# A ring of four patch buffers for the gathers of a deformable convolution, filled a pair of blocks ahead

## The reference, cut to what matters

```
def reference(x, ...):                       # x: 8 x 256 x 128 x 128, float32
    x = x + L0(groupnorm(x))                 # layer 0
    x = x + L1(groupnorm(x))                 # layer 1
    return x

def L0(x, offset_w, offset_b, mod_w, mod_b, kv_w, kv_b, out_w, out_b):
    offsets = conv2d(x, offset_w, offset_b, 1)             # 3x3, 8 channels
    mod = 1.0 + tanh(conv2d(x, mod_w, mod_b, 1))           # 3x3, 4 channels
    v = conv2d(x, kv_w, kv_b, 0)[:, C:]                    # 1x1, 256 channels
    # px, py: each pixel's own place plus its offsets, one pair for each of 4 groups
    sampled = bilinear(v, px, py) * mod                    # four corners, weighted
    return conv2d(sampled, out_w, out_b, 0)                # 1x1

def L1(x, weight, bias):                     # whitening in 16 groups of 16 channels
    xg = (x - mean(x)) in groups
    cov = xg xg^T / M + 1e-4 I
    return (cov^(-1/2) xg) * weight + bias
```

## Time and profile before

| | us |
|---|---|
| median of 3 timed runs | 6903.72 |
| lowest, highest | 6898.48, 6908.78 |
| span of the profiled execution | 7542.0 |
| GpSimd busy in it | 4578.9 (61%) |
| TensorE busy (matmul) | 4572.0 (61%) |
| VectorE busy | 4223.0 (56%) |
| ScalarE busy | 1067.2 (14%) |

### The profile page before, as it was taken

How to read it: one execution, slowest core, us unless ns; L and a number is a source line. 1 busy time by engine, 2 the same in 40 slices (tenths; PEclk the granted TensorE clock), 3 DMA queues, 4 the chain that set the end, 5 groups by cost and what they waited for, 6 DMA issues and landing times.

```text
span 7542.0 us, 73500 instructions
## 1 busy us (share of the span) xinstructions
PE 4572.0 (61%) x17916; PEld 2935.6 (39%) x17916; DVE 4223.0 (56%) x8110; ACT 1067.2 (14%) x2723; POOL 4578.9 (61%) x4115
## 2 busy tenths in 40 slices
PE   5765656565566656655665656566665544446777
PEld 3443434344344433333443434343443333234322
DVE  6655656555565555555655556555555544345555
ACT  1211111111111111111111111111111111010000
POOL 0377667676767767667676677676776777770000
PEclk9877778787788878777887878787887766667999
DMA  8866657666666666666666666565565544445999
GB/s 283 275 203 212 200 185 227 195 205 201 197 206 207 209 194 208 197 193 207 202 216 196 201 206 217 188 216 186 184 195 183 187 131 136 129 129 193 421 421 412
DMA packets 1069670, 1612.36 MB, mean 214 GB/s; under 512 B 92080, under 2 KB 617008, under 8 KB 1067568
## 3 DMA queue, kind: packets, MB, share of 16 engines
q0 software_dynamic: 196608, 537.13, 22.2%
q10 hardware_dynamic: 632832, 536.91, 22.0%
q1 hardware_dynamic: 240176, 537.77, 20.7%
HBM read 1074.58 MB, written 536.87 MB: 214 GB/s over the span
## 4 chain that ended last, share of the span: by engine, by line
another core or an unknown queue 21%; issue 21%; PE 19%; DVE 18%; DMA 9%; POOL 5%; DVEq 3%; ACT 3%; ACTq 1%; POOLq 0%; SPq 0%
PE psA L929 6%; DVE patch L568 5%; PE psO L965 5%; POOL patch L829 5%; DMA out_dram<-vring 4%; DVE patch L570 4%; PE psG L994 3%; DMA vring<-x 3%; PE psT L954 2%; DVE xr L582 2%; DMA v<-vring 1%; DVE vring L483 1%; PE psT L979 1%; DVE bst L418 1%
## 5 line engine op out<-in xcount | busy, mean ns | idle before, releaser
L829 POOL DMA_INDIRECT patch<-v,index_now x4096 | 4572.9, 1116 | 2224.0 <-issue 1517.0
L568 DVE TENSOR_TENSOR patch<-patch,weight 128x2048 f32<-128x2048 f32 x512 | 1171.3, 2288 | 941.4 <-DMA patch<-v,index_now 553.1
L929 PE MATMUL psA<-wB,xa 128*128 128x364 f32 x3824 | 1498.5, 529 | 185.2 <-DVE taps L486 103.1
L979 PE MATMUL psT<-ident,xr 128*128 128x128 f32 x2048 | 373.8, 343 | 1712.3 <-issue 928.5
L582 DVE SCALAR_TENSOR_TENSOR xr<-psO,bo_sb,xr 128x512 f32<-128x512 f32 x512 | 375.2, 748 | 1205.9 <-remote 972.5
L979 PEld LDWEIGHTS psT<-ident,xr 128*128 128x128 f32 x2048 | 300.6, 177 | 1917.7 <-issue 1067.8
L965 PE MATMUL psO<-sampT,wO_sb 128*128 128x512 f32 x2048 | 985.3, 626 | 73.4 <-issue 42.1
L929 PEld LDWEIGHTS psA<-wB,xa 128*128 128x128 f32 x3824 | 769.6, 218 | 574.4 <-issue 208.8
L954 PE MATMUL psT<-ident,samp 128*128 128x128 f32 x2048 | 409.9, 329 | 674.2 <-DVE samp L573 440.1
L1126 ACT ACTIVATE x1T<-psT 128x512 f32<-128x512 f32 x512 | 290.0, 596 | 3629.8 <-PE psT L979 1597.1
L994 PE MATMUL psG<-x1T 128*128 128x129 f32 x4096 | 664.6, 329 | 29.8 <-issue 18.7
(11 more groups left out here) (176 smaller groups left out, 2935.5 us busy)
## 6 DMA issues: line engine op xcount, KB each, us to landing
v<-vring ACTq DMA_DIRECT2D x256, 1024.0 KB
xa<-x_dram SPq DMA_DIRECT2D x256, 512.0 KB
xr<-x_dram SPq DMA_DIRECT2D x256, 512.0 KB
x<-xr ACTq DMA_DIRECT2D x256, 512.0 KB
xs<-x_dram SPq DMA_DIRECT2D x224, 512.0 KB
taps<-x SPq DMA_DIRECT2D x96, 1024.0 KB, 13.4
out_dram<-taps ACTq DMA_DIRECT2D x96, 1024.0 KB, 18.9
patch<-v,index_now POOLq DMA_INDIRECT x4096
```

The source lines that it names most:

```text
L568: eng.tensor_tensor(v4, v4, w4, ALU.mult).then_inc(weighted, 1)
L829: eng.indirect_dma_start(out=patch[j][:, t, :], out_offset=None, in_=v2_flat[k], in_offset=bass.IndirectOffsetOnAxis(ap=index_now[j][:, t: ...
L929: mm = eng.matmul(conv_bank[wide][r][:, 0:NA], xa[j][:, c, r * W:(r + 1) * W], wB[:, c, :], start=(c == 0), stop=(c == CC - 1))
L979: mm = eng.transpose(psT[h][:, at:at + P], xr[j][:, c, row * W:(row + 1) * W], ident[:, :])
```

## The change

`patch` and `index_now` become rings of four (`RING`), numbered n = 2m + j, where m is the parity of the pair. The index copies of pair i+1 are issued on ScalarE at the head of pair i, block by block, ahead of the x1 store and of the sample copies. The semaphores `sampled` start at 2 where they started at 1, so that gathers and index copies of a pair wait for the samples of the pair before last; `got` has eight members. As `samp[j]` is no longer protected by the gathers' wait, VectorE waits for ScalarE's copies (`psT_free`) before it writes the first half of a block; `psT_free` starts at 4. The three operations of the weighted sum stay as they are.

To make room, `taps` shrinks from 130 rows to two strips of 10 rows, one for each parity of the pair: 8 rows of its own and one row of each neighbour. VectorE writes the first and the last row of a pair a second time into the other strip. The buffers of the last stage move into patch buffers 2 and 3 and the memory of `xa` and `xs`. In the first stage the offsets are issued between conv rows 2 and 3 of the second block. All loops over pairs run over two pairs at a turn.

```
-        taps = sb("taps", [P, H + 2, NT])
+        taps = sb("taps", [P, 2, QR + 2, NT])
-        index_now = [sb(f"index_now{j}", [P, NJ], U32) for j in range(2)]
-        patch = [sb(f"patch{j}", [P, NJ, PATCH]) for j in range(2)]
+        index_now = [sb(f"index_now{n}", [P, NJ], U32) for n in range(RING)]
+        patch = [sb(f"patch{n}", [P, NJ, PATCH]) for n in range(RING)]
...
         def pairs(eng, pair):
-            pair(0)
-            with eng.Fori(1, PAIRS - 1) as i:
-                pair(i)
-            pair(PAIRS - 1)
+            pair(0, 0, 0)
+            with eng.Fori(0, PAIRS // 2 - 1) as h:
+                pair(eng.snap(h * 2 + 1), 1, h)
+                pair(eng.snap(h * 2 + 2), 0, eng.snap(h + 1))
+            pair(PAIRS - 1, 1, PAIRS // 2 - 1)
...
# VectorE, conv_out
+                    if row == 0 and top:
+                        eng.memset(taps[:, 1 - m, QR + 1, :], 0.0)
+                        eng.memset(taps[:, m, 0, :], 0.0)
+                    elif row == 0:
+                        eng.tensor_tensor(taps[:, 1 - m, QR + 1, :], bank[:, C:NA], biasB[:, C:NA],
+                                          ALU.add)
+                    elif row == QR - 1:
+                        eng.tensor_tensor(taps[:, 1 - m, 0, :], bank[:, C:NA], biasB[:, C:NA],
+                                          ALU.add)
+                    eng.tensor_tensor(taps[:, m, row + 1, :], bank[:, C:NA], biasB[:, C:NA], ALU.add)\
...
# VectorE, sample
-                eng.wait_ge(halved, (b * PAIRS + i) * 4 + 2 * j + h + 1)
+                eng.wait_ge(halved, half)
+                if h == 0:
+                    eng.wait_ge(psT_free[CC - 1], (b * PAIRS + i) * 4 + 2 * j + SAMP_FREE - 3)
...
# GpSimd
+            for free in (*sampled[0], *sampled[1]):
+                eng.sem_inc(free, 2)
+            for free in psT_free:
+                eng.sem_inc(free, SAMP_FREE)
...
+                n = 2 * m + j
                 eng.wait_ge(sampled[j][1], b * PAIRS + i + 1)
                 eng.wait_ge(index_cp, (b * PAIRS + i) * 2 + j + 1)
...
-                        out=patch[j][:, t, :], out_offset=None, in_=v2_flat[k],
+                        out=patch[n][:, t, :], out_offset=None, in_=v2_flat[k],
...
-                    with eng.Fori(0, PAIRS) as i:
-                        for j in range(2):
-                            gather(b, k, i, j)
+                    with eng.Fori(0, PAIRS // 2) as q:
+                        for m in range(2):
+                            for j in range(2):
+                                gather(b, k, q * 2 + m, m, j)
...
# TensorE, first stage
-                            conv(range(ROWS))
-                            if j == 1:
-                                offsets(a, i, s is not None)
+                            if j == 0:
+                                conv(range(ROWS))
+                            else:
+                                conv((0, 1, 2))
+                                offsets(a, i, m, s is not None)
+                                conv((3,))
...
# ScalarE, pair
                     for j in range(2):
+                        if not last:
+                            if g is not None:
+                                indices(g, i + 1, 1 - m, j)
+                        elif a is not None:
+                            indices(a, 0, 0, j)
                         if g is not None:
                             if j == 1:
                                 x1_store(g, i, 0)
...
                             samples_out(g, i, j)
-                        if not last:
-                            if g is not None:
-                                indices(g, i + 1, j)
-                        elif a is not None:
-                            indices(a, 0, j)
```

More of the change, by code:

```diff
@@ L53 @@
 NH = NJ // 2
+RING = 4
+SAMP_FREE = 4
 S0 = 4 * BP
@@ L143, in deform_zca_kernel @@
         pm = {n: sb("p_" + n, [P, QR, G]) for n in ("tm", "th", "w0", "w1", "ia")}
+        xa = [xa_mem[:, j, :, :] for j in range(2)]
+        xs = [xs_mem[:, j, :, :] for j in range(2)]
         psA = [ps(f"psA{i}") for i in range(2)]
@@ L469, in prep, with conv_out @@
                 eng.wait_ge(psI_free, b * NU + 3)
-            def conv_out(b, i, j, rows, wide):
+            def conv_out(b, i, m, j, rows, wide):
+                top = ends(i)[0]
                 for r in rows:
-                    k = r % 2
+                    k, row = r % 2, j * ROWS + r
                     eng.wait_ge(row_full[j][r], b * PAIRS + i + 2)
@@ L610, in pair @@
                     prepare = last and ca is not None
+                    if last and a is not None and s is None:
+                        eng.memset(taps[:, m, QR + 1, :], 0.0).then_inc(edge, 1)
                     for j in range(2):
                         if g is not None:
-                            sample(g, i, j, 0)
+                            sample(g, i, m, q, j, 0)
                             if j == 1:
@@ L931, in conv_rows, with offsets @@
                     mm.then_inc(row_full[j][r], 1)
-            def offsets(b, q, more):
+            def offsets(b, q, m, more):
+                bottom = ends(q)[1] and not more
                 for k in range(2):
-                    eng.wait_ge(psA_free[k], (b * PAIRS + q) * 4 + 5 + (0 if ends(q)[1] else 2))
+                    eng.wait_ge(psA_free[k], (b * PAIRS + q) * 4 + (5 if bottom else 7))
+                if bottom:
+                    eng.wait_ge(edge, 1)
                 eng.wait_ge(psI_free, offsets_use(b, q, more))
```

87 lines of the change are left out of this document (44 added, 43 removed).

## The result

| | before | after |
|---|---|---|
| median of the timed runs, us (9 each) | 6900.76 | 6918.52 |
| lowest, highest | 6886.09, 6908.78 | 6910.33, 6926.74 |
| span of the profiled execution | 7542.0 | 6925.0 |

The ratio is 1.0025 with an interval of 1.0015 to 1.0034: slower by 18 us. The forecast was 6893, which was 11 us less than the 6904 known then. The profile lost 617 us and the median gained 18. From the page of the changed kernel, first the shares of the chain by engine, then two of the costliest groups (count | busy us, mean ns | idle before, releasers).

The account below looks back on a forecast made before the run. GpSimd's issuing of gathers was taken as the bound. The median 6904 less 18 of waits, plus 5 of meetings and 2 of additions, gave 6893 us, bounds 6867 to 6920; the 8-in-10 range was 6790 to 6945.

Parts of the forecast that it names:

- The reading of the chain: Gather stage: GpSimd's issuing of gathers is the chain, 4572.9 us busy, 1237.2 of pauses and 707.0 of waits for index copies.
- C: Rival, gather stage: all waits are real and recording slows GpSimd's pace; time 6290 us; chance 0.16.
- B: Rival, gather stage: some waits are real, as at image changes, 20 to 110 us saved; time about 6840; chance 0.27.
- D: Rival, pair loops: GpSimd pays 0.4 to 1.9 us at each of 64 turns of doubled bodies; slower, up to 7008 us; chance 0.15.
- Part of the recording: Gather stage: the 675 us of waits for index copies come from profiling and are nearly absent in timed runs.
- first term: Ring of four, gather stage: removes all waits for index copies, 0 to 37 us in the timed runs, 18 taken.
- meetings: Multiplies that lengthen gathers once GpSimd never pauses: 0 to 83 us more in the profile; 0 to 8 timed, 5 taken.
- 675: GpSimd's waits for the index copy in the profile before: 707.0 us less the ordinary pauses in 105 waits.
- Second term: First stage, TensorE: offsets ahead of conv row 3; row 3 some 2 us later, placement some 2 us earlier; cost nothing.
- 2 us, at most 8: First stage, VectorE: two more additions of 0.26 us for each pair, from the taps in two strips; 2 us taken.
- The rule held against the rows: VectorE and GpSimd port lock: by the skill's rule the halving and last addition would lose 983 us; the row shows none.

Follow-up runs that it names:

- the first experiment: The kernel before, unchanged, recorded and timed once more: 7459.1 us, 0.9967 of the kernel before, with a recorded span of 7462.8 us.
- the copy of before: The kernel before, unchanged, under another name, recorded where the kernel before took 6904.0 us: 6909.8 us, ratio 1.0011, recorded span 6898.2 us.
- The second comparison: The changed kernel timed again beside the kernel before (6903.0 us): 6909.6 us, ratio 1.0013.

## Why the prediction was right or wrong

**The reading of the chain was right.** The waits went from 707.0 to 0.6 us, and the span came out at 6925 where 6867 to 6950 was the sum; the mean gather is 1134 ns (forecast 1116 to 1136) and the stage 5900 us (5840 to 5930). The profile gained 8% and the median nothing. C falls: it had the waits in the timed runs too, and the old kernel's record at 6898.2 us has none, at the gathers' usual pace (a median of 946 ns). The same pace in the two first profiles, 947 ns against 949, would not have told, as both are recorded. B falls too, for the undisturbed record of before holds no wait over 0.3 us; those of 4.54 and 1.74 us at a change of images were disturbance too. D falls by its mechanism: behind the first gather no pause of GpSimd is over 0.32 us in the record after, at a turn of the loop or elsewhere, while 60 packets of instructions were moved instead of 42. That the sign is D's is a coincidence.

**"Part of the recording" was wrong.** I took the disturbance for something that the profiler does, since the timed runs lacked it. The runs show timed executions with it (7387 to 7647 us) and records without it (6898.2). The consequence for the median was the same; the reason, "what recording would do and no data path of this kernel does", was argued from slow register instructions and fell at the first experiment.

**The failed step of the median, first term: "they hold between 0 and 37 us of waits; I take 18".** There were none. The 37 us above 6867 were meetings, and the text had the price in hand. A record without waits has the meetings that the waits had covered, priced there at 0 to 83 us. The measured difference of the gathers is 4631.8 - 4572.9 = 59 us. Then 6867 + 59 = 6926 is the old kernel undisturbed, the measured span 6898, and nothing is left over for waits. The other 28 us show that 675 was too small as well: the pauses between gathers come to 2224.0 - 279.8 = 1944 us in the profile before and to 1528.5 - 281.1 = 1247 in the undisturbed record, which is 697 us of disturbance; 22 of it stood in the row "issue". The last 6 us lie outside the stage of gathers. I added the meetings to the new kernel in the profile's sum and forgot them in the old kernel's own time. Without this slip the forecast is 6904 + 2, and a gain isn't among the likeliest cases. The 5 us of added meetings fall with the waits.

**Second term: the order of the first stage, priced "Nothing".** The sentence said "row 3 some 2 us later and the placement some 2 us earlier". The first half came, the second is wrong: on VectorE the placement stands behind row 3, so it begins 2.1 us after the offsets' end instead of 0.04. Behind it the next block's banks come free late, and TensorE waits for them. TensorE is busy 0.96 of the time there once the first loads are in, which the mean over 290 us (199 of 290) hid, so that the waits push everything behind. The first gather of the changed kernel starts 8 us late in undisturbed sets (298.8 against 290.9) and 14.4 against the same kernel with the old order. "2 us, at most 8" was set aside for the additions, which proved to be hidden altogether.

**What is left.** In the undisturbed records the last gather starts where the first one's start, the gathers' busy time and 1247 us of pauses add up to. Between the copy of before and the first record of the changed kernel that start moves by 6191.0 - 6169.1 = 22 us: 8.7 from the first gather, 12.9 from gathers held longer. In the second record of the changed kernel it moves by 1.3 us: 7.9 from the first gather, 6.8 back from gathers held less. So the 8 us stand in both, and how long the multiplies hold the gathers scatters by 20 us between two records of one kernel (4644.7 and 4625.0), more than the whole 18 us. The second comparison gave 1.0013, 7 us, and a copy of before 1.0011. That the change costs some 8 us in the median is likely from the rows, but no median shows it; the rest is open, and scatter of the holding is my guess.

**The rule held against the rows.** I let refute it: "the row shows none of it". The rule is true here for VectorE's side. That one gather ends inside the halving shows nothing, since it had begun before the halving did, and the holds by the multiply put the next gather at the very end of the halving, too late to be lengthened. The 983 us that I worked out as its price was wrong as well: it took every microsecond of the halving as lost, though gathers under way at that time lose nothing. As the Trainium skill says (SBUF — State Buffer, section SBUF: two separate sides), the lock is exclusive, for a VectorE operation with two SBUF inputs too, and held for the whole instruction. The trace agrees where VectorE comes first, with a gather's end 0.82 us past the end of either operation. Where the gather comes first it doesn't: by that page VectorE would wait for the rest of the gather's 0.95 us, and the longest of 512 multiplies took 2.37 us instead of 2.29. Read that way it would have pointed at the cut of the multiply, worth 495 us.

**What stays open.** What the disturbance is; why it comes with some sets and not others on the same chip; why the ring and the split lose more in it. Seen are only register instructions of 0.7 us on VectorE and SP, and stretches of up to 46 us in which every engine but GpSimd stands while gathers go on. The disturbed records also hold fewer semaphore events, 36 to 43 thousand against 104 to 105 thousand in the others, so what a wait there is put down to is less sure than its length. That goes for the 707.0 us of the earlier trace rows too.

## What to carry to other kernels

Before waits of a profile are priced, hold its span against the timed median of the same kernel. Where the two differ by about as much as the waits that are to go, get a second record of the old kernel first, and price into its own time whatever the waits had covered. When steps change places on one engine, follow the step that moves back through the engine that works on it next: what stands behind it there moves back too. And where one engine's long instruction holds another engine's short ones, cut the long one in two before adding buffers: here that gave 7%, and four buffers nothing.

## What the hardware did that I had not expected

A gather of 0.947 us that begins inside a VectorE operation with two SBUF inputs, more than some 0.05 us after its start, ends 0.82 us after it; one already under way isn't touched, and hardly touches the operation. Two parts of 1024 elements cost 2.36 us instead of 2.29 and bring the lengthening of all gathers from 4644.7 - 4096 x 0.947 = 766 to 4113.8 - 4096 x 0.946 = 239 us.

The same kernel took 6904 or 7464 to 7610 us by the set of runs. In the slower kind single register instructions take 0.7 us instead of 0.08 and the gathers keep their 946 ns. The two kinds put the same kernels into opposite order: 0.928 and 1.106 for one.
